# Two-layer graph attention block: projections in plain fp32 instead of three float32r products, and attention logits made from unsplit fp32 terms in row tiles

## The reference, cut to what matters

```python
# layer 0: six heads of 64, masked softmax
q, k, v = heads(x @ Wq + bq), heads(x @ Wk + bk), heads(x @ Wv + bv)
probs = softmax(q @ k.T / 8 + where(adj, 0, -9e15))
x1 = layernorm(x + (probs @ v) @ Wf + bf)
# layer 1: twelve heads of 32, additive logits, gated output
h = x1 @ W                                    # 128 x 384, twelve heads
src, dst = tanh(h) @ w_src, tanh(h) @ w_dst   # one number per node and head
attn = softmax(where(adj, leaky_relu(src[n] + dst[m], 0.2), -999))
f = elu(attn @ h + b)
gate = sigmoid(x1 @ H_w.T + H_b)
out = layernorm(x1 + gate * f + (1 - gate) * x1)
```

## Time and profile before

| | us |
|---|---|
| median of three runs | 1132.66 (1132.14 to 1134.66) |
| the profiled execution | 1132.1 |
| its span in the trace | 1130.2 |
| busy in the span: PE, PEld | 1073.2, 883.3 |
| busy: ACT, DVE, POOL | 919.4, 897.2, 765.2 |
| iterations 2 to 15, about | 925 |

### The profile page before, as it was taken

How to read it: one execution, slowest core, us unless ns; L and a number is a source line. 1 busy time by engine, 2 the same in 40 slices (tenths; PEclk the granted TensorE clock), 3 DMA queues, 4 the chain that set the end, 5 groups by cost and what they waited for, 6 DMA issues and landing times.

```text
span 1130.2 us, 25501 instructions
## 1 busy us (share of the span) xinstructions
PE 1073.2 (95%) x8236; PEld 883.3 (78%) x8236; DVE 897.2 (79%) x1828; ACT 919.4 (81%) x3383; POOL 765.2 (68%) x909
## 2 busy tenths in 40 slices
PE   6889999999999999999999999999999999997774
PEld 5678888888888888878888888888888888786652
DVE  5457878888887888888788888878888887888874
ACT  3348888888888888888888888888888888888874
POOL 1367776676777667677766767776676777667652
PEclk9999999999999999999999999999999999999986
DMA  9101010020101002010100201010020101000000
GB/s 270 56 2 57 15 68 18 8 71 16 64 15 61 26 8 71 16 64 15 62 26 8 71 15 64 15 60 27 8 72 16 64 15 43 16 8 16 16 15 21
DMA packets 25893, 44.66 MB, mean 40 GB/s; under 512 B 2462, under 2 KB 23714, under 8 KB 25762
## 3 DMA queue, kind: packets, MB, share of 16 engines
q1 hardware_dynamic: 23234, 41.91, 10.9%
q10 hardware_dynamic: 2496, 1.12, 0.5%
q0 software_dynamic: 32, 0.00, 0.0%
HBM read 30.43 MB, written 12.58 MB: 38 GB/s over the span
## 4 chain that ended last, share of the span: by engine, by line
PE 57%; POOL 23%; issue 9%; DVE 6%; ACT 3%; DMA 2%; POOLq 0%; ACTq 0%; DVEq 0%
PE ps_b L253 13%; PE ps_d L253 13%; POOL z L964 9%; PE ps_a L253 7%; PE ps_d L459 5%; POOL xT_lo L916 4%; PE ps_a L382 3%; PE ps_s L362 3%; PE ps_s L354 3%; PE ps_d L447 3%; POOL p L991 3%; PE ps_c L469 2%; POOL s L956 2%; POOL thw L999 2%; POOL y L958 2%
## 5 line engine op out<-in xcount | busy, mean ns | idle before, releaser
L583 ACT ACTIVATE z<-z,s 128x128 f32<-128x128 f32 x768 | 297.1, 391 | 1.5 <-DVE s L798 0.9
L964 POOL TENSOR_TENSOR z<-z,mask 128x512 f32<-128x512 f32 x192 | 218.2, 1164 | 0.5 <-ACT z L679 0.5
L583 ACT ACTIVATION_READ_ACCUMULATOR z<-z,s 128x1 f32 x768 | 146.6, 191 | 0.0
L610 ACT ACTIVATE p<-ps_s,s 128x128 f32<-128x128 f32 x384 | 134.7, 378 | 13.1 <-DVE s L776 13.0
L991 POOL TENSOR_TENSOR p<-p,s 128x768 f32<-128x768 f32 x64 | 94.2, 1471 | 61.4 <-DVE s L804 61.4
L459 PE MATMUL ps_d<-ident,z 128*128 128x128 f32 x768 | 118.7, 278 | 9.2 <-ACT z L583 8.2
L953 POOL TENSOR_SCALAR s<-s 128x1 f32<-128x1 f32 x128 | 28.8, 225 | 143.3 <-DVE s L895 131.6
L999 POOL TENSOR_TENSOR thw<-th,w_sd 128x768 f32<-128x768 f32 x64 | 117.4, 1834 | 3.7 <-ACT th L633 3.7
L459 PEld LDWEIGHTS ps_d<-ident,z 128*128 128x128 f32 x768 | 90.6, 143 | 17.6 <-ACT z L583 9.1
L679 ACT ACTIVATE z<-ps_d 128x512 f32<-128x512 f32 x192 | 100.8, 598 | 1.2 <-PE ps_d L447 1.2
L945 POOL TENSOR_TENSOR xb<-xb,bf_all 128x768 f32<-128x768 f32 x32 | 58.6, 1834 | 58.6 <-DVE sd L878 55.5
(11 more groups left out here) (154 smaller groups left out, 3448.5 us busy)
## 6 DMA issues: line engine op xcount, KB each, us to landing
x_cols<-in_xT_dram SPq DMA_DIRECT2D x16, 768.0 KB, 6.4
xb<-in_x_dram SPq DMA_DIRECT2D x16, 768.0 KB, 4.9
out_dram<-y SPq DMA_DIRECT2D x64, 192.0 KB, 1.8
z<-in_L_gnn_Wq_dram SPq DMA_DIRECT2D x1, 576.0 KB, 6.4
p1T<-in_L_gnn_Wk_dram SPq DMA_DIRECT2D x1, 576.0 KB, 8.7
qT<-in_L_gnn_Wv_dram SPq DMA_DIRECT2D x1, 576.0 KB, 11.1
kT<-in_L_gnn_Wf_dram SPq DMA_DIRECT2D x1, 576.0 KB, 13.4
z<-in_L_gnn_W_dram SPq DMA_DIRECT2D x1, 576.0 KB, 11.7
```

What stands on the lines that cost most here:

```text
L583: done = act.activation(z[:, a, :], z[:, a, :], ACT.Exp, bias=neg1[:, a:a + 1], accum_out=sum1[:, a:a + 1])
L610: last = act.activation(p0[:, o, i, :], ps_s[:, o, i * N:(i + 1) * N], ACT.Exp, bias=neg0[:, k:k + 1], accum_out=sum0[:, k:k + 1])
L964: pool.tensor_tensor(z[:, 4 * q:4 * q + 4, :], z[:, 4 * q:4 * q + 4, :], mask[:, t, :].unsqueeze(1).broadcast_to([P, 4, N]), ALU.add).then ...
```

## The change

All weights, x, x1 and the context are held once, in fp32, and each chunk product is one fp32 matmul. The copies to `_hi` become copies to the one tensor; all `_lo` work and the weights' staging go. x lands directly in one of two buffers in turn. `sd` is laid out in six blocks of 32 columns with ones beside the four terms of a bank, so that two fp32 transposes of 96 columns (to free columns of `ps_c` and `ps_a`) give both operands; the logits are three fp32 matmuls of 32 rows each, in row tiles 0, 32 and 64. `rows_L` is one ACT copy; the five splitting operations and two one-time fills of constants go.

```diff
-            def split_product(out_ap, lhs, rhs, chunks=range(C), closed=True):
+            def product(out_ap, lhs, rhs, chunks=range(C), closed=True):
                 for c in chunks:
-                    for k, (a, b) in enumerate(HI_LO):
-                        last = pe.matmul(out_ap, lhs(a, c), rhs(b, c), start=(c == 0 and k == 0),
-                                         stop=(closed and c == C - 1 and k == 2))
+                    last = pe.matmul(out_ap, lhs(c), rhs(c), start=(c == 0), stop=(closed and c == C - 1))
...
-                for c in range(C):
-                    for k in range(2):
-                        last = pe.matmul(ps_s[:, 0, 0:D], bv_col[:, c:c + 1].broadcast_to([P, P]),
...
+                    last = pe.matmul(ps_s[:, 0, 0:D], bv_col[:, c:c + 1].broadcast_to([P, P]),
+                                     weights["wf"][:, c, :], start=(c == 0), stop=(c == C - 1))
...
-                pe.wait_ge(S["sd3_ready"], t + 1)
-                pe.transpose(ps_t, sd3_wide[:].rearrange("p s w -> p (s w)"), ident_b[:]).then_inc(S["sd_turned"], 1)
+                pe.wait_ge(S["sd_ready"], t + 1)
+                pe.transpose(ps_rows, sd_rows, ident[:]).then_inc(S["sd_turned"], 1)
+                pe.transpose(ps_cols, sd_cols, ident[:]).then_inc(S["sd_turned"], 1)
...
+                pe.wait_ge(S["rows_ready"], t + 1)
                 for q in range(3):
-                    pe.wait_ge(S["rows_ready"], 3 * t + q + 1)
+                    tile = slice(32 * q, 32 * (q + 1))
                     if due(t):
                         pe.wait_ge(S[f"p1T_{q}"], t)
                     heads = ps_d[:, q, :].rearrange("p (a n) -> p a n", a=4)
-                    last = pe.matmul(heads, rows_L[:, q, :], cols_R[:], start=True, stop=True)
+                    last = pe.matmul(heads, rows_L[tile, :], cols_R[tile, :, :], start=True, stop=True)
...
-                        for q in range(3):
-                            act.activation(rows_L[0:64, q, :], ps_t[0:64, :], ACT.Copy, scale=of_bank[0:64, q:q + 1]
-                                           ).then_inc(S["rows_ready"], 1)
+                        act.activation(rows_L[0:96, :], ps_rows, ACT.Copy).then_inc(S["rows_ready"], 1)
...
-                        sp.wait_ge(S["x_lo"], xb_and_x_lo)
-                    sp.dma_start(x_cols[:], following).then_inc(S["x_in_ready"], 16)
+                    if g > 0:
+                        sp.wait_ge(S["v_made"], G * g)
+                    sp.dma_start(xT[:, 1 - par, :, :], xT_in[g + 1]).then_inc(S["x_odd_in" if g % 2 == 0 else "x_even_in"], 16)
...
-                    if gat:
-                        lo_part(x1T, ps_b, slice(0, N), "x1_hi", tl + 1, "x1_lo")
...
-                    if qkv and n + 1 < NG and j == 3:
-                        x_lo(g + 1, 0)
-                        x_lo(g + 1, 1)
```

More of the change, by code:

```diff
@@ L32 @@
 F32 = mybir.dt.float32
-F32R = mybir.dt.float32r
 BF16 = mybir.dt.bfloat16
@@ L70, in build_program @@
         ident_b = sb("ident_b", [P, P], BF16)
[L71 to L74, removed]
+        of_slot = sb("of_slot", [P, 4])
+        rows_L = sb("rows_L", [P, N])
+        cols_R = sb("cols_R", [P, 4, N])
         ones_b = sb("ones_b", [P, P], BF16)
@@ L89, in build_program @@
         mask = sb("mask", [P, B, N], BF16)
-        x_cols = sb("x_cols", [P, C, G * N])
-        xT = [sb("xT_hi", [P, C, G * N], F32R), sb("xT_lo", [P, C, G * N], F32R)]
+        xT = sb("xT", [P, 2, C, G * N])
         xb = sb("xb", [P, 2, G, D])
@@ L100, in build_program @@
         p0T = sb("p0T", [P, 2, C, N])
-        ctxT = [sb("ctxT_hi", [P, C, N], F32R), sb("ctxT_lo", [P, C, N], F32R)]
+        ctxT = sb("ctxT", [P, C, N])
         r0 = sb("r0", [P, D])
@@ L106, in build_program @@
         x1 = sb("x1", [P, 2, G, D])
-        x1T = [sb("x1T_hi", [P, C, N], F32R), sb("x1T_lo", [P, C, N], F32R)]
+        x1T = sb("x1T", [P, C, N])
         h = sb("h", [P, 2, H1, D1])
@@ L394, in project_out @@
                         pe.wait_ge(S["r0_ready"], t)
-                    pe.wait_ge(S["ctx_lo"], t + 1)
+                    pe.wait_ge(S["ctx_ready"], t + 1)
                     if n == 1 and j == 0:
-                        pe.wait_ge(S["weight_lo"], 4)
-                last = split_product(ps_b[:, 0:D], lambda a, c: ctxT[a][:, c, :],
-                                     lambda b, c: w_parts["wf"][b][:, c, :], chunks)
+                        pe.wait_ge(S["weight_in_3"], 16)
+                last = product(ps_b[:, 0:D], lambda c: ctxT[:, c, :], lambda c: weights["wf"][:, c, :], chunks)
                 if chunks[-1] == C - 1:
@@ L637, in iteration @@
                         evacuate_v(2)
-                    if qkv and n + 1 < NG and j == 3:
-                        x_hi(g + 1, 1)
                     if att:
@@ L853, in iteration @@
                         evacuate_v(3)
-                    if n == 0 and j < 3:
-                        weight_parts(3 + j)
                     if n == 0 and j == 3:
@@ L1042 @@
     held["ident"] = _np.eye(P, dtype=_np.float32)
[L1043 to L1047 removed]
+    row = _np.arange(P)
+    held["pick"] = ((row % 32 < 8)[:, None] & (row[:, None] % 4 == _np.arange(4)) & (row < 96)[:, None]
+                    ).astype(_np.float32)
     arrays, args = {}, []
```

199 lines of the change are left out of this document (61 added, 138 removed).

## The result

The changed kernel takes 1277.4 us (median of four runs, 1276.6 to 1278.5) against 1132.4 for the kernel before on the same chip: ratio 1.128, interval 1.126 to 1.130, or 145 us slower. The prediction said 1262, in a range of 1240 to 1292. The profiled execution took 1278.5 us, its span 1276.7.

The account below looks back on a forecast made before the run. The prediction took PE, fed without a gap at full clock, as the bound. Its terms gave +2.17 us a graph, +121.5 for 56, plus 2.9 and 5.2 elsewhere: 1262 us, 11% slower, range 1240 to 1292.

Parts of the forecast that it names:

- PE's products: Chunk products, fp32 for three float32r matmuls: 0.116 more per 384 columns, 0.167 per 512; +2.14 us a graph.
- what PE gets back: First matmul behind a transpose or tiled matmul: its excess, seen as an unhidden weight load, goes; -0.46 us a graph.
- the logits, with the wait ahead: Three fp32 matmuls in row tiles, running side by side: 1.33 us instead of 1.00, +0.33 a graph.
- turning the terms: Two fp32 transposes, 0.22 us, where one bf16 transpose cost 0.06: +0.16 us a graph.
- Rival (b): First matmul behind transposes: its cost stays, +0.46 x 60 = +28 us, 1290 us in all; chance 9%.
- The stagger of the third tile: Logits: the third tile waits for ACT's copy of p1T_2 and starts about 0.25 us late.
- What is worth nothing in the stretch: Stage with all parts: low-part work on POOL and DVE and two ACT copies lie beside PE; removing them gains nothing.
- Start and end: Outside the 56 full graphs: start about 0, iteration 1 +5.2 us, iteration 16 +2.9, last two graphs cancel.
- (a): Logits: the row tiles don't overlap, 2.80 instead of 1.33 us, +93 us, 1355 us in all; chance 7%.
- (c): PE: weight loads set its pace, so fewer loads make the kernel faster, about 1048 us; chance 4%.
- (d): Whole kernel: no change, the 2.17 us a graph vanishing in PE's gaps; chance 1%.
- (e): PE meets a new wait, such as the third bank or cols_R; each 0.3 us a graph +19, 1270 to 1310; 10%.

Follow-up runs that it names:

- e2: Kernel before with each chunk product as one fp32 matmul of the hi parts, low parts still made but unused: 1254.3 us, 1.107.
- e1: Kernel before with only the new sd, transposes, rows_L, cols_R and logits, and the old products: 1159.4 us, 1.024.
- e3: Kernel before with only the q and k products as one fp32 matmul of the hi parts: 1171.7 us, 1.035.
- e7: Kernel before with one float32r matmul (hi times hi) for each chunk product, low parts still made: 1127.8 us, 0.996.
- e6: Changed kernel with all three logits matmuls on the 32 rows of tile 0: 1413.4 us, 1.248 to the kernel before.
- e8: Kernel before with only the gate's products cut to one float32r matmul (hi times hi): 1129.3 us, 0.997.
- e4: Kernel before with the three gate chunks in one block behind turn_p0 instead of between the transposes: 1195.1 us, 1.055.

## Why the prediction was right, and which term was off

Per full graph, from the start-to-start table (three q or k graphs and one v graph to a group):

| step of the prediction | predicted | measured |
|---|---|---|
| PE's products | +2.14 | +2.13 |
| what PE gets back | -0.46 | 0 |
| the logits, with the wait ahead | +0.33 | +0.31 |
| turning the terms | +0.16 | +0.15 |
| a wait ahead of `turn_p0` in the old kernel, gone | none | -0.08 |
| sum | +2.17 | +2.51 |

**PE's products** held: 0.323 per record of 384 columns and 0.43 of 512. The first q or k block with `turn_x1` ahead grew by 0.49, three times 0.164 (0.167 predicted), `project_h` by 0.35, three times 0.117 (0.116). The upper bound, which was taken for 512 columns, was the right one.

**What PE gets back** is the step that failed. It took the longer first float32r matmul behind a transpose (429 against 338 ns) for a weight load that can't hide, and its -0.46 made 56 x 0.46 = 26 us of the forecast. Between starts no such cost exists. Before, four transposes and a gate or output chunk took 0.36 + 0.61 = 0.97 us; after, 0.44 + 0.65 = 1.09. That is the plain +0.12 of a product. In the old kernel the longer record starts early, beneath the last transpose: its block is 0.36 long there and 0.44 with an fp32 matmul behind it. e2, with the old transposes and fp32 products, has 0.44 as well. The 91 ns more of span were overlap, and taking them away gave nothing. That the sum of the means of spans was used for a cost, when the same text says that spans overlap and durations must be read from starts, was the mistake. Rival (b), for which the cost stays, names the term that failed. Its 1290 is 13 us too high, by the other terms below, and its reason is not what the runs show, since there was no cost. Behind the context, in column tiles, the first product takes 0.11 longer than one in a row before and 0.10 after. So that excess did not go either; whether it is a cost or another overlap stays open.

**The logits.** The tiles run side by side, as the scores did. The stagger of the third tile was 0.1 us and not 0.25, and 0.09 stands between the last output product's own 0.65 and the logits. The third tile starts 0.05 us after ACT's copy of its bank ends, here and in e1. In e1, where the last output chunk is shorter and covers less of that copy, the stagger is 0.18 and the logits take 1.23. So the stagger is real and depends on what stands ahead.

**A wait that the waits hardly show.** In one graph of four of the kernel before, the last matmul of the second q or k block has 0.42 to 0.64 us to the next start instead of 0.23. The timeline of PE before, at one of them:

```profile
498.07 0.40 PE L253 MATMUL ps_b<-xT_lo,wq_hi 128*128 128x512 f32 x1
498.60 0.88 PE L362 MATMUL ps_s<-ident,p 128*128 128x128 f32 x6
```

`turn_p0` waits for `p` there, by 0.3 us, of which the matmul's span of 0.40 covers more than half; so the waits count only 1.4 us for all of them. The start is 0.05 us after POOL ends `p`; in the other graphs it is 0.66 us or more behind. With longer products the wait is gone. This is 0.08 a graph, and 0.3 of e3's missing 0.5 a group. It was the visible end of the loop that e7 showed.

**What is worth nothing in the stretch** held, by e1 + e2 against the whole: a group takes 76.1 us by either. **Start and end** were predicted at +8.1 outside the 56 graphs and came to +5.8 (2.4 + 3.4); iteration 16 grew by 0.9 a graph and not 0.73, as it should without the 0.46 and with its waits for POOL. So the miss of 17 us in the span (146.5 against 129.6) is 26 for the get-back, less 7 for the other terms of a graph (0.12 x 56), less 2 outside. That the time fell within the range is thus partly luck: the wait that went was not foreseen, and it and the smaller misses hid 9 of the 26 us.

**The rivals.** (a) Tiles one after the other: refuted by the trace; with all in one tile e6 took 1413, more than the 1355 given for it, and 36 of that is the lower clock. (c) The weight loads set the pace: refuted; they fell from 83% to 60% of the stretch and it became 15% longer. (d) No change: refuted. (e) A new wait: refuted. PE's waits have no rows from 105 to 1155 us. Short waits would have none, but the steps add up to the terms above, and no step varies by more than 0.002 us.

What the prediction said without having shown it is that PE alone bounded the kernel before. For a change that makes PE longer that is enough, and e1, e2 and e3 follow PE's own list to within a few us. For one that makes PE shorter it would have failed, as e7 and e8 show.

## What to carry to other kernels

Cost a matmul by the distance of starts in an unbroken row of its kind, and never by the mean of spans: a longer record at a seam can be overlap that costs nothing and can't be won back. An engine that never waits is a bound against which growth counts in full, but that says nothing of what shrinking it would bring: taking 1.05 us a graph from PE brought 4 us of 67 (e8), with the clock at 1.00. The shares of the chain that ended last had shown it (PE 57% before, 93% after). Where such a balance holds, the order of the filling work is worth more (63 us in e4) than its amount. And an engine that is made to wait can be granted a lower clock behind the wait, in which its own part of the loop gets longer, as in e7.

## What the runs showed of the hardware that was not expected

Three fp32 matmuls of 32 rows and 512 columns in three row tiles took 1.16 us from their first start to the next instruction's, against 2.77 in one row tile, 2.4 times as long. Each matmul's two records stand together on PE's list, yet the first records of all three tiles start within 0.11 us, and the second ones 0.53 later.

With all three in one tile (e6) the granted clock fell 21 times to its lower level, 0.50, with PE never idle, each time less than 0.9 us behind the 2.77 us of 32-row matmuls. That cost 36 us. It did not fall once in the stage with all parts of the changed kernel, where the same work takes 1.16 us. In e7 it stood at the lower level behind a wait of PE of 2.01 us.
